# Two-layer expert network with a mixer and a pooling layer: the expert products and their gelu handed over by halves of 512 tokens

## What is computed

```
x = x + state_space_mix(layernorm(x))                    # "a": projections, a state per head, output product
t = t + moe(layernorm(t), 8 experts, hidden 128)         # "b": layer 0
x = x + x_n / sqrt(pool_k(x_n^2) + pool_3x3(x_n^2) + c)  # "c": x_n = layernorm(x), then scale and offset
t = t + moe(layernorm(t), 8 experts, hidden 256)         # "d": layer 1

def moe(xf):                       # every expert on every token
    w = top-2 gate weights         # zero for the other six experts
    for e in range(8):
        h = gelu(xf @ W1[e] + b1[e])
        out += w[:, e] * (h @ W2[e] + b2[e])
```

## Time and profile before

| | before |
|---|---|
| device time, median of 3 runs | 530.72 us (529.05 to 530.82) |
| the profiled execution | 529.8 us, of which the profile's span is 528.0 us |
| busy: TensorE / weight loads | 459.3 us (87%) / 242.0 us (46%) |
| busy: VectorE / ScalarE / GpSimd | 397.6 / 364.4 / 254.4 us (75 / 69 / 48%) |
| the chain that ended last | TensorE 57%, VectorE 15%, ScalarE 11%, issue 8%, GpSimd 6% |

### The profile page before, as it was taken

One profiled execution on the slowest core, in us unless ns is written; L12 is line 12 of the kernel. 1 busy time (PEld: TensorE's weight loads), 2 busy tenths in 40 slices (PEclk: granted clock), 3 DMA queues, 4 the chain that ended last, 5 costly groups with the idle time before them and its releaser, 6 DMA issues.

```text
span 528.0 us, 12523 instructions
## 1 busy us (share of the span) xinstructions
PE 459.3 (87%) x4978; PEld 242.0 (46%) x4978; DVE 397.6 (75%) x832; ACT 364.4 (69%) x445; POOL 254.4 (48%) x217
## 2 busy tenths in 40 slices
PE   0557948954999999999999999999999999899995
PEld 0443534433465445544654455545544444345342
DVE  6766586897889888988898888887968576666332
ACT  2235538444788987998689959896879687786751
POOL 3320463382447373936392648444754453435224
PEclk9999977965999999999999999999999999999999
DMA  7000702500581047302840085006600760240150
GB/s 261 21 2 4 180 1 71 113 2 1 121 185 40 2 98 181 89 1 65 187 117 1 24 190 121 15 4 163 160 23 0 165 160 21 65 100 21 51 128 24
DMA packets 17305, 42.03 MB, mean 80 GB/s; under 512 B 2656, under 2 KB 7904, under 8 KB 17120
## 3 DMA queue, kind: packets, MB, share of 16 engines
q1 hardware_dynamic: 16608, 39.13, 30.5%
q0 software_dynamic: 640, 2.10, 1.3%
HBM read 38.60 MB, written 2.62 MB: 78 GB/s over the span
## 4 chain that ended last, share of the span: by engine, by line
PE 57%; DVE 15%; ACT 11%; issue 8%; POOL 6%; DMA 1%; POOLq 0%; SPq 0%; DVEq 0%; ACTq 0%
PE hP L847 22%; PE yP L866 21%; PE sA L698 7%; PE sC L698 4%; ACT H L684 3%; ACT L684 3%; ACT L573 2%; POOL ACC L550 2%; PE sA L705 1%; POOL stat_n L515 1%; DVE nacc L1155 1%; POOL stat_b L492 1%; DVE YW L1199 1%; DMA WB<-w_scratch 1%; PE sA L756 1%
## 5 line engine op out<-in xcount | busy, mean ns | idle before, releaser
L684 ACT ACTIVATE H<-hP,K 128x1024 f32<-128x1024 f32 x192 | 210.8, 1114 | 58.5 <-PE hP L847 56.3
L847 PE MATMUL hP<-xT,w 128*64 128x512 f16 x1536 | 204.4, 389 | 8.1 <-ACT H L684 8.1
L866 PE MATMUL yP<-H,w 128*64 128x512 f32 x768 | 197.5, 594 | 1.5 <-DVE YW L1199 0.8
L550 POOL TENSOR_TENSOR ACC<-ACC,YW 128x512 f32<-128x512 f32 x96 | 131.9, 1385 | 137.9 <-DVE YW L1199 137.4
L847 PEld LDWEIGHTS hP<-xT,w 128*64 128x64 f16 x1536 | 85.8, 112 | 119.4 <-issue 60.1
L1199 DVE SCALAR_TENSOR_TENSOR YW<-yP,K,WB 128x512 f32<-128x512 f32 x96 | 71.3, 746 | 35.7 <-PE yP L866 28.4
L866 PEld LDWEIGHTS yP<-H,w 128*64 128x64 f32 x768 | 51.8, 137 | 30.1 <-issue 7.0
L1155 DVE SCALAR_TENSOR_TENSOR nacc<-PAD,K,nacc 128x528 f32<-128x528 f32 x56 | 45.5, 812 | 1.4
L515 POOL TENSOR_TENSOR stat_n<-stat_n,neg_half 128x8 f32<-128x8 f32 x8 | 13.7, 1710 | 38.4 <-DVE stat_n L1103 38.4
L1199 DVE SCALAR_TENSOR_TENSOR ACC<-yP,K,WB 128x512 f32<-128x512 f32 x32 | 23.2, 744 | 11.5 <-DMA WB<-w_scratch 7.3
L573 ACT ACT_TABLE_LOAD x21 | 26.9, 1283 | 3.4 <-DVE nacc L1155 3.0
(11 more groups left out here) (151 smaller groups left out, 621.1 us busy)
## 6 DMA issues: line engine op xcount, KB each, us to landing
WB<-w_scratch SPq DMA_DIRECT2D x128, 256.0 KB, 5.4
X<-in_x SPq DMA_DIRECT2D x8, 256.0 KB, 5.9
out<-X POOLq DMA_DIRECT2D x8, 256.0 KB, 3.0
WB<-in_m_W SPq DMA_DIRECT2D x1, 1024.0 KB, 9.4
WB<-in_m_W SPq DMA_DIRECT2D x1, 512.0 KB, 6.7
w<-in_m_W SPq DMA_DIRECT2D x1, 512.0 KB, 10.0
w_scratch<-wTs SPq DMA_DIRECT2D x16, 32.0 KB, 2.1
K<-in_consts SPq DMA_DIRECT2D x1, 453.5 KB, 7.2
```

The costliest lines, as they stand in the source:

```text
L550: pool.tensor_tensor(ACC[ACC_OF[m]][:, cols], ACC[ACC_OF[m]][:, cols], YW[:, u % 4, :], ALU.add).then_inc(summed, 1)
L684: nc.scalar.activation(H[:, s % RING, :], hP[s % 2][:, :], ACT.Gelu, bias=b1[l][:, e * ch + c:e * ch + c + 1], scale=1.0 / WS)\
L847: mm = nc.tensor.matmul(hP[s % 2][b * C:(b + 1) * C, hf * HALF:(hf + 1) * HALF], w1[l][:, sp, w, b * C:(b + 1) * C], xT[l][g % 2][:, hf * ...
L866: mm = nc.tensor.matmul(yP[hf][a * C:(a + 1) * C, :], w2[l][:, (2 * j + a) * ch + c, :], H[:, (2 * ch * j + 2 * c + a) % RING, hf * HALF:( ...
```

## The change

Three things change. The first product of a slot is ordered by halves of the tokens (first all four matmuls of tokens 0 to 511, then four of 512 to 1023), and each half waits for its own half of the gelu two slots before and signals by itself. The gelu of a slot is two instructions of 512 tokens, each with its own wait and signal. The second product waits for the half of the gelu that it reads. And all tables of places have new numbers, `AB_SHIFT`, `CD_SHIFT` and `CD_LEAD` too, which move whole groups of steps.

```diff
                 if s < E * ch:
                     tables[0] = None
                     n = CHUNK_BASE[m] + s
-                    act.wait_ge(h_ready, n + 1)
...
-                    nc.scalar.activation(H[:, s % RING, :], hP[s % 2][:, :], ACT.Gelu,
-                                         bias=b1[l][:, e * ch + c:e * ch + c + 1], scale=1.0 / WS)\
-                        .then_inc(gelu_done, 1)
+                    for hf in range(2):
+                        cols = slice(hf * HALF, (hf + 1) * HALF)
+                        act.wait_ge(h_ready, 2 * n + hf + 1)
+                        nc.scalar.activation(H[:, s % RING, cols], hP[s % 2][:, cols], ACT.Gelu,
+                                             bias=b1[l][:, e * ch + c:e * ch + c + 1], scale=1.0 / WS)\
+                            .then_inc(gelu_done, 1)
...
-                    if n >= 2:
-                        pe.wait_ge(gelu_done, n - 1)
...
-                    for sp in range(2):
-                        for hf in range(2):
+                    for hf in range(2):
+                        if n >= 2:
+                            pe.wait_ge(gelu_done, 2 * (n - 2) + hf + 1)
+                        for sp in range(2):
                             for b in range(2):
                                 mm = nc.tensor.matmul(hP[s % 2][b * C:(b + 1) * C, hf * HALF:(hf + 1) * HALF],
...
-                    mm.then_inc(h_ready, 1)
+                        mm.then_inc(h_ready, 1)
...
-                    pe.wait_ge(gelu_done, CHUNK_BASE[m] + 2 * ch * j + 2 * c + 2)
+                    pe.wait_ge(gelu_done, 2 * (CHUNK_BASE[m] + 2 * ch * j + 2 * c + 1) + hf + 1)
...
-    cd=dict(turn_c=13, pool0=15, turn_u=23, turn_d=28, gate=29, send=34),
+    cd=dict(turn_c=15.5, pool0=16.5, turn_u=22.5, turn_d=29.5, gate=31, send=37),
...
-CD_SHIFT = (0, 0, 0, 0, 0, 0, 0, -4)
-CD_LEAD = 1.5
+CD_SHIFT = (0, 0, 0, 0, 0, 0, -5, -7)
+CD_LEAD = 1
```

More of the change, by code:

```diff
@@ L58 @@
 PE_AT = dict(
-    ab=dict(turn_a=4, proj0=6.5, proj1=8, proj2=8.5, state=20.5, mixer=22.5, y0=23.5, y1=24.5, y_sums=25.5,
-           mix_out=27, turn_b=34.5, gate=38, send=43),
-    cd=dict(turn_c=13, pool0=15, turn_u=23, turn_d=28, gate=29, send=34),
-    final=(14.5, 15.5, 22.5, 26))
+    ab=dict(turn_a=3.5, proj0=5.5, proj1=10, proj2=12, state=19.5, mixer=20.5, y0=22, y1=23, y_sums=24,
+           mix_out=25.5, turn_b=38.5, gate=40, send=43),
+    cd=dict(turn_c=15.5, pool0=16.5, turn_u=22.5, turn_d=29.5, gate=31, send=37),
@@ L63 @@
+    final=(14.5, 15.5, 24.5, 26.5))
 ACT_AT = dict(
-    ab=dict(sums_a=-15.5, turn_a=5, proj0=6, proj1=8, proj2=8.5, decay=11.5, y0=23, y1=23.5, sums_b=27.5, turn_b=34,
-           top2=40.5, send=42),
-    cd=dict(sums_c=8, turn_c=12.5, norms=21, sums_d=24, turn_d=27.5, top2=29.5, send=34),
+    ab=dict(sums_a=-6.5, turn_a=4, proj0=8.5, proj1=9.5, proj2=11.5, decay=15.5, y0=21.5, y1=21.5, sums_b=29.5,
+           turn_b=39, top2=40, send=41.5),
+    cd=dict(sums_c=11, turn_c=15, norms=20, sums_d=23.5, turn_d=29.5, top2=31, send=36.5),
@@ L67 @@
     final=NO_FINAL)
 DVE_AT = dict(
[L69 to L73, removed]
+    ab=dict(centre_a=-13, sums_a=-5.5, norm_a=-3.5, decay=13.5, values=18, state=19, mixer=20.5, y_sums=23,
+           mix_out=25.5, centre_b=29, sums_b=31, norm_b=33.5, top2=40.5, weights=40.5),
@@ L74 @@
+    cd=dict(centre_c=10.5, sums_c=13, norm_c=14.5, pool0=17, pool1=17, pool2=17, pool3=18.5, turn_u=23.5,
+           centre_d=23.5, sums_d=24, norm_d=27.5, top2=31, weights=33.5),
+    final=(14.5, 16, 24.5, 27.5))
 POOL_AT = dict(
-    ab=dict(sums_a=-7.5, norm_a=-5.5, state=24, y_sums=25, sums_b=32.5),
-    cd=dict(sums_c=9.5, norm_c=18, scale=19.5, sums_d=25.5),
+    ab=dict(sums_a=-10, norm_a=-2, state=16, y_sums=20, sums_b=30.5),
+    cd=dict(sums_c=8, norm_c=19.5, scale=19.5, sums_d=24),
@@ L77 @@
     final=NO_FINAL)
 SP_AT = dict(
-    ab=dict(decay=-12.5, send=30.5),
-    cd=dict(send=38.5, piece1=48, piece2=39.5, piece3=41),
+    ab=dict(decay=4.5, send=37.5),
+    cd=dict(send=38, piece1=48, piece2=53, piece3=53),
     final=NO_FINAL)
-STORE_AT = 29.5
+STORE_AT = 32.5
 AB_LEAD = 40.5
@@ L91, in moe_start @@
     return moe_start(1, g - 1) + E * CHUNKS[1]
[L94 to L96 removed]
+AB_SHIFT = (-1, -1, 0, 0, 0, 0, 0, 0)
+CD_SHIFT = (0, 0, 0, 0, 0, 0, -5, -7)
+CD_LEAD = 1
 def ab_start(g):
@@ L624, in ab @@
                     if g >= 2:
-                        act.wait_ge(h_ready, CHUNK_BASE[(0, g - 2)] + E)
+                        act.wait_ge(h_ready, 2 * (CHUNK_BASE[(0, g - 2)] + E))
                     evacuate_T("b", g, sA16, xT[0][g % 2][:, :])
@@ L659, in cd @@
                     if g >= 2:
-                        act.wait_ge(h_ready, CHUNK_BASE[(1, g - 2)] + 2 * E)
+                        act.wait_ge(h_ready, 2 * (CHUNK_BASE[(1, g - 2)] + 2 * E))
                     evacuate_T("d", g, sC16, xT[1][g % 2][:, :])
```

## The result

The changed kernel takes 547.27 us in the median, the kernel before 530.77 us in the runs beside it: ratio 1.0295, 95% interval 1.0257 to 1.0334. It is 3% slower. One of the four runs of the changed kernel took 1625.4 us; it is in the median and not in the ratio. The prediction said 532.0, within 525 to 540. The profiled execution of the changed kernel took a span of 545.5 us, against 528.0 before.

A forecast was written before the change was run, and what follows sets the result against it. TensorE was taken to bound the middle. Profiled: 529.8 + 6.7 (five periods) - 3.5 (ahead) - 1.9 (behind) = 531.1 us; the median of runs is 0.9 above, so 532.0, range 525 to 540.

The forecast's parts named there:

- the one on VectorE in the middle: Full period, scaled product behind the taps: VectorE and TensorE arrive together, 0.2 us of wait, 0 to 1.3 possible.
- periods of 56.4: Sign for the forecast: full periods in the middle take 56.4 us, with TensorE idle near 2.4 us in each.
- if they pass 57, the one on VectorE: Sign in the full periods: if they pass 57 us, the step on VectorE's place is wrong.
- The rival that VectorE takes the middle: Full periods: taps in one piece hold the scaled products, another 1.1 us each; start gives only 1; 540.0 us, chance 0.18.
- the sixth group's earlier place: Near the end: its gate moves 3.5 slots ahead, its loads are met by other work, waits of 0.41 and 1.37 us go.
- Ahead of the periods: Where the periods begin: first gelu some 3.5 us earlier, taken as -3.5 us; bounds 0 and the whole 4.3 us wait.
- the prediction's test: Start of the periods: first product of the first period's slots about 4 us earlier, the wait before L727 gone.
- Behind them: After the periods: one longer wait, +1.1, against four waits gone or shrunk; together -1.9 us, from +1.1 to -3.3.
- the wait for WB: Near the end, TensorE's wait for the turned weights: grows from 0.66 us to some 1.7, about 2 as a sign.
- The gelu by halves: ScalarE, every slot: a half takes 699 ns, two halves 1.20 us against 1.01 whole, 4.6 us more a period.
- The gate product: Full period, gate product of layer 0: TensorE waits 0.8 us for ScalarE's copy behind loads and four gelu halves.
- the first product behind the second loads: Full period, behind the second pair of table loads: TensorE waits 1.2 us, and 0.2 more for the second half.
- The extra wait a slot: TensorE, every slot: one more wait by halves, taken as nothing; 192 exposed ones would cost 11.5 us.

The follow-up runs named there:

- sums_thin: Changed kernel with GpSimd's additions cut to 64 of 512 columns, leaving out seven eighths of the experts' sum: 527.72 us, ratio 0.9951.
- port_tail: Kernel before plus a tail of four VectorE instruction forms, alone, then beside 16 GpSimd additions: product 0.68 to 1.74 us, cast 0.42 to 1.48, other two unchanged.
- halves_whole_gelu: Kernel before with only signals and waits by halves, every gelu in one step: 531.77 us, ratio 1.0030.
- GpSimd later: Changed kernel with three GpSimd steps put later (sums_c 5 slots, sums_a 4.5, y_sums 3.5): 545.25 us, ratio 1.0262.

## Why the prediction was wrong

**The failed step is the one on VectorE in the middle**: "From the gate product to the scaled product behind the taps I add up 20 us of VectorE work ... The two arrive together, so I put 0.2 us there". Measured: 1.38 us in each of the three middle periods and 0.33 at the next second product. The sum took every VectorE instruction at its undisturbed time, although the trace of before had one that was held (`xcen`, 1.11 us at 245.33). In the changed order `xcen` and its cast take 3.04 us and not 1.12, since GpSimd's additions run beside them; that is 1.92 us more, ahead of a wait of 1.38. With the additions cut the wait is 0.15 and a period 56.5, the prediction's "periods of 56.4" (sums_thin); the form-by-form run shows the same two forms held and the others not (port_tail). Its own test, "if they pass 57, the one on VectorE", named the right engine. The rival that VectorE takes the middle had the place and, at 540.0, the side; it counted on more work and had no word for an instruction that is held.

This step is not the whole miss. By its sum the span should have grown by 1.3 us, and it grew by 17.5. Of the 16.2 between them 4.5 are this step's (1.5 in each middle period), 5.4 the last period's, 1.1 the first period's, 3.5 those that the start did not give and 1.8 those that the end did not; the parts are rounded.

The Trainium skill has the rule, and the prediction did not use it: "SBUF — State Buffer", section "Who interferes with whom", says that a VectorE instruction with two inputs in SBUF, or one in a two-port mode such as a cast may enter, contends with a GpSimd instruction that reads SBUF, and that one with at most one SBUF input outside those modes does not. The trace agrees in each of the four forms.

**The last period** cost 6.7 us more than before. The prediction priced the sixth group's earlier place by what it frees at the end and never by what it lands on. There it lands `xnrm` on three piled-up additions: 3.91 us of wait, which falls with their number (1.52 with one addition beside it) and with their length (2.30 at 256 columns, none at 64). The stretch of half clock behind the wait adds 1.7. Being held was at nothing in the sum here as in the middle, and so was the clock.

**Ahead of the periods** it had -3.5 and got 0. The products did come earlier: the wait before L727 is gone and the first product of the slots starts at 127.0 and not 130.0, as the prediction's test asked. The prediction also named what the first gelu waits for, `top2` and `weights` of layer 1, a centring, three small operations more and the exponential of layer 0's gate. Its error is the size: "Behind them I get the first gelu some 3.5 us earlier". VectorE and ScalarE, in the kernel before and, in the second fence, after:

```profile
123.92 0.23 DVE L997 SCALAR_TENSOR_TENSOR gt<-sC,K 128x64 f32<-128x64 f32 x1 [1.66 <-PE sC L698]
...
130.73 0.26 ACT L588 ACTIVATE gt<-gt 128x64 f32<-128x64 f32 x1 [0.38 <-DVE gt L1003]
...
132.30 1.11 ACT L684 ACTIVATE H<-hP,K 128x1024 f32<-128x1024 f32 x1
```

```profile
124.10 0.22 DVE L999 SCALAR_TENSOR_TENSOR gt<-sC,K 128x64 f32<-128x64 f32 x1
...
130.69 0.26 ACT L588 ACTIVATE gt<-gt 128x64 f32<-128x64 f32 x1 [2.31 <-DVE gt L1005]
...
132.26 1.27 ACT L686 ACTIVATE H<-hP,K 128x512 f32<-128x512 f32 x2
```

The chain on VectorE begins at the same time, is as long (6.8 and 6.6 us), and the first gelu starts at the same time in both. It stood behind that chain before too, so moving the product won nothing. This is read from the two traces; no run tried it. The clock adds to it: in the kernel before TensorE has its full clock from 134.0 on, in the changed one from 138.5, after a wait of 2.35 us for that gelu between its first products. The first period begins inside this stretch of 0.50, which costs about 1.8 of the 2.5 us that it lost (an estimate from the starts of its products, twice as far apart as at full clock).

**Behind them** it had -1.9 and got -0.1. The waits of 0.41, 1.37 and 0.90 are gone as foretold, and the wait for WB is 1.09 at TensorE, where 1.7 was foretold. Four new things take it back: the next group's `xnrm` 1.59, its `zT` 1.83 where 0.58 stood, 0.31 for a scaled product, and half clock from 483.2 to 486.7, behind the wait for `zT`, about 1.7.

**What held.** The gelu by halves: 384 rows of 691 ns (699 foretold), 0.58 us apart where they follow each other (0.60 foretold). ScalarE is busy 48.96 us of a period (50.3 foretold) and does not bound it. The figures that the prediction takes from the Trainium skill, "ScalarE: Activation LUTs", section "What ACT_TABLE_LOAD costs", give 280 - 93 = 187 ns for a pair of halves over a whole, not its 0.22 us; the traces have 2 x 0.58 - 1.00 = 0.16. The gate product waits 0.62 (0.8 foretold), the first product behind the second loads 1.39 with its half (1.4 foretold). The extra wait a slot was put at nothing; with whole gelus it costs 0.2 us in a period (halves_whole_gelu), where 24 exposed ones would cost 1.4.

Not settled: how much of the 17.5 us each place gives back if moved alone. Putting steps back one at a time made new waits each time, and the sixth group's shift was not undone under the new tables.

## What to carry to other kernels

Add up a busy engine's work with the durations of the order that will run: a two-operand SBUF instruction or a cast that comes to stand beside GpSimd's work takes 1.4 to 1.7 us where it took 0.4 to 0.7, and a step placed early on an in-order queue makes what piles up behind it run in one block, where it may hurt most. Where a trace names a releaser, see whether the waiting instruction reads it at all; here the true one was on another engine and ended 0.14 us before. The places of a hand-made order are no sum of parts (one part moved into the old order or out of the new one cost 8 to 41 us in seven of eight runs), while the halves alone, in the old places, take 0.3% off, with an interval that reaches no change; no version here that does the whole work is faster. And price a wait of the engine with the clock: behind some waits it works at half clock, which cost 1.7 us twice in the changed kernel.

## What the runs showed of the hardware

VectorE's pair `xnrm` was held through three additions of GpSimd in a row (4.75 us for 0.76, the additions 3.70, their usual 1.23 each), while in the tail the two engines took turns (1.74 and 1.5 us on either side). Being held is therefore not always for one instruction of the other engine. What decides which of the two happens, no run here shows.

TensorE's granted clock fell to 0.50 within about 2 us of the end of waits of 3.91 and 1.83 us in the changed kernel, 1.76 us with the additions on 64 columns, and 4.06, 2.26 and 2.22 us in the run with the shift of four slots. It stayed at 1.00 behind waits of 2.12 us (halves alone) and 1.52 us (GpSimd later). No run here was made to separate what brings it down.
